# One scan over both row blocks of a pair, and the FFN's units carried on around the out-projection, in a decoder layer on one core

## The chip, the cores and the metric

One core of a Trainium2 chip. The metric is device time in microseconds of one execution of the whole program. TensorE multiplies matrices into PSUM, ScalarE applies functions with a per-partition scale and bias, VectorE and POOL (GpSimd) do elementwise work, and SyncE issues the DMAs. Each engine runs its own instructions in order and waits on semaphores.

## The reference

A decoder layer with three sublayers, each followed by a residual sum and a layer norm, on x of 2 x 2048 tokens x 512:

```python
xz = x @ W_in + b_in;  u, z = silu(first half), silu(second half)      # 1024 channels each
B, C = split(u @ W_xproj + b_xproj);  dt = softplus(u @ W_dt + b_dt)    # 16 states
h = h * exp(dt * A) + (dt * u) * B        # per token, channel and state, in order of time
y = (sum over states of h * C + D * u) * z
x = layernorm(x + y @ W_out + b_out)
x = layernorm(x + cross_attention(x, context of 77 tokens, 16 heads, mask))
hidden = x @ W1 + b1                      # 2048
q = hidden + gain * sin(theta + 0.1 * hidden);  x = layernorm(x + relu(q) @ W2 + b2)
```

## The kernel before

**The scan part** (`selective_scan_phase`). The 4096 tokens are cut into 8 time chunks of `TS` = 512; four chunks make a sequence. In a chunk the 1024 channels x 16 states are 128 row blocks of 128 rows, taken two at a time: 64 pairs a chunk, 512 in all, and every engine's program is one loop over `pair`. The two blocks of a pair lie side by side in PSUM and SBUF, 512 columns each. For one pair:

- TensorE spreads dt over states into `r_ps` (`rep_dt`, L361, four matmuls of 32 rows) and dt*u into `u_ps` (`rep_dtu`, L374). `r_ps` holds two pairs, `u_ps` one.
- ScalarE makes exp(dt*A) in place in `r_ps` (`exps`, L599, one ACTIVATE per block, since the scale differs).
- VectorE multiplies `u_ps` by B into `h` (`dbu`, L743, 1024 columns at once) and runs the recurrence (`scans`, L756, one scan per block, start value from `carry` or zero).
- ScalarE saves the last column of both blocks (`save_carry`, L605), for this pair of the next time chunk; POOL then multiplies `h` by C (`weigh`, L852).
- TensorE sums over states every second pair (`sums`, L390) and, in every fourth of those, adds the D*u row by an identity matmul (L398).

`h` is a ring of three groups of two pairs. The order on the engines is written by hand. TensorE's turn for `pair` is `rep_dtu(pair + 2)`, `produce`, an out-tile's half in the last chunk, `sums`, `rep_dt(pair + 2)`. `produce` holds the projections of the next time chunk, cut by the class `Plan` into 6 or 9 matmuls of 512 columns a pair (L40 to L42 on `pj`, one PSUM bank that ScalarE evacuates). ScalarE's turn is evacuations, `save_carry(pair)`, `exps(pair + 2)`, then Silu with its table loads, softplus and fp16 halves. VectorE's turn is `dbu(pair + 1)`, `scans(pair)`, and a `gate` every eighth pair. In the last chunk pairs 32 to 63 also carry half an out-projection tile each (`out_piece`, 12 matmuls).

**The attention and FFN part** (`attention_ffn_phase`) goes over 16 token chunks of 256. Body c holds the attention of chunk c and the FFN of chunk b = c - 1, and chunks 1 to 6 (`ops`) also the out-projection of two tiles of a later chunk: 48 matmuls of 512 columns into `sps`, the same PSUM that the scores use. The FFN has 8 units: `hidden(b, n)` (24 matmuls of 256 columns), ScalarE's `hid_out`, VectorE's `fraction`, ScalarE's `sine`, VectorE's `mix`, ScalarE's `relu`, VectorE's `act_low`, then `second(b, n)` on TensorE (24 matmuls of 512 columns). ScalarE's `out_evacuated` (L1447) empties the out-projection, VectorE's `masked` (L1710) reads the scores. POOL adds biases (`o_bias`, `x1_bias`, `x1_sum`, `x2_bias`) and makes the low half of y (`y_low`, L1900). Chunk 1 is special (`late` is false): weights are still being split there, and its out-projection's second tile needs `y_low(5)`.

## Time and profile before

| what | value |
|---|---|
| median of 3 runs | 3168.35 us (3167.78 to 3171.23) |
| profiled execution | 3163.83 us |
| its span | 3162.1 us |
| mean granted clock of TensorE | 0.966 |
| scan part: first and last scan start | 59.0 and 1962.9 us |

The span runs from the first to the last instruction of the profiled execution; a clock of 1.0 is 2.4 GHz, 0.5 is 1.2 GHz. Work on an engine that is not waited for costs nothing, so the table says little without the order of waits.

### The profile page before, as it was taken

Reading aid. Unit: us, or ns where it says so; the run is one execution under the profiler, and the core shown is the slowest. Engines: PE = TensorE matmul, PEld = TensorE weight load, DVE = VectorE, ACT = ScalarE, POOL = GpSimd, SP = SyncE. Lnnn points to the kernel's source line nnn. Section 1 sums busy time; section 2 is a strip of 40 time slices with the busy share of each in tenths; the row PEclk is TensorE's granted clock in tenths of the full one; section 3 lists DMA queues with packets and bytes.
Section 4 is the critical chain, followed back from the end, with each engine's and each line's share of the span. In section 5 each row is a group of like instructions: output and inputs, shape, how many; then the busy total and the mean of one; then the engine's idle time right before and its main releaser. Section 6 shows DMA issues by size and latency. Waiting matters only on the chain. (4 is left out here: it accounts for less than half of the span.)

```text
span 3162.1 us, 48953 instructions
## 1 busy us (share of the span) xinstructions
PE 2830.4 (90%) x18968; PEld 1268.4 (40%) x18968; DVE 2692.5 (85%) x3070; ACT 2015.1 (64%) x3616; POOL 1828.9 (58%) x944
## 2 busy tenths in 40 slices
PE   7878878978878888888889889989999999999998
PEld 2222222222222222222222223556666676667765
DVE  5899999999999999999999978766666677777776
ACT  6766776776776776776776745555555556655564
POOL 4788988978978988978988987311111111112100
PEclk9999999999999999999999989999999999999999
DMA  4111112112112111111112143701111000000000
GB/s 159 51 51 41 58 51 66 45 37 71 41 43 65 41 51 57 50 41 57 51 53 65 51 131 125 225 28 42 42 42 42 28 29 22 23 30 29 30 8 14
DMA packets 119976, 172.51 MB, mean 55 GB/s; under 512 B 13250, under 2 KB 48706, under 8 KB 119236
## 3 DMA queue, kind: packets, MB, share of 16 engines
q1 hardware_dynamic: 119748, 169.37, 16.5%
q8 instruction: 155, 2.54, 0.3%
q14 instruction: 73, 0.60, 0.1%
HBM read 100.66 MB, written 66.58 MB: 53 GB/s over the span
## 5 line engine op out<-in xcount | busy, mean ns | idle before, releaser
L852 POOL TENSOR_TENSOR h<-h,c_rep 128x1024 f32<-128x1024 f32 x511 | 1196.7, 2355 | 281.6 <-ACT carry L605 280.1
L756 DVE TENSOR_TENSOR_SCAN h<-r_ps,carry,h 128x512 f32<-128x512 f32 x768 | 938.9, 1262 | 10.6 <-ACT r_ps L599 10.4
L599 ACT ACTIVATE r_ps<-r_ps,decay 128x512 f32<-128x512 f32 x1024 | 631.7, 656 | 390.3 <-PE r_ps L361 389.8
L743 DVE TENSOR_TENSOR h<-u_ps,b_rep 128x1024 f32<-128x1024 f32 x512 | 614.0, 1199 | 48.0 <-PE u_ps L374 47.4
L374 PE MATMUL u_ps<-dtu,spread 32*128 32x512 f16 x2048 | 319.5, 390 | 105.3 <-DVE h L743 105.0
L361 PE MATMUL r_ps<-dt,spread 32*128 32x512 f16 x2048 | 316.9, 387 | 49.7 <-DVE h L756 43.1
L390 PE MATMUL y_ps<-h,gather 128*32 128x512 f32 x2048 | 288.4, 637 | 65.8 <-POOL h L852 64.7
L1882 POOL TENSOR_TENSOR o_in<-o_in,rows 128x1024 f32<-128x1024 f32 x15 | 37.0, 2464 | 508.9 <-DMA o_in<-o_dram 508.9
L756 DVE TENSOR_TENSOR_SCAN h<-r_ps,zero,h 128x512 f32<-128x512 f32 x256 | 313.1, 1263 | 7.1 <-ACT r_ps L599 7.0
L40 PE MATMUL fps<-x,region 128*128 128x256 f16 x1024 | 283.6, 277 | 3.4 <-issue 2.4
L41 PE MATMUL fps<-x,region 128*128 128x256 f16 x1024 | 283.0, 276 | 0.0
L42 PE MATMUL fps<-x,region 128*128 128x256 f16 x1024 | 282.8, 276 | 0.0
L40 PE MATMUL pj<-x_high,region 128*128 128x512 f16 x484 | 194.5, 402 | 39.3 <-ACT u L517 18.6
L361 PEld LDWEIGHTS r_ps<-dt,spread 32*128 32x128 f16 x2048 | 58.2, 93 | 392.5 <-DVE h L756 206.9
L1900 POOL TENSOR_TENSOR y<-y_t,y 128x1024 f16<-128x1024 f32 x13 | 28.3, 2180 | 318.8 <-ACT y L1440 318.8
L40 PE MATMUL pj<-u_high,region 128*128 128x512 f16 x504 | 199.4, 396 | 1.7 <-ACT soft L572 1.4
L40 PE MATMUL nat<-region,act 128*128 128x512 f16 x512 | 194.1, 379 | 7.1 <-DVE act L1695 5.8
L41 PE MATMUL pj<-u_low,region 128*128 128x512 f16 x504 | 197.4, 392 | 0.0
L42 PE MATMUL pj<-u_high,region 128*128 128x512 f16 x504 | 197.1, 391 | 0.0
L42 PE MATMUL nat<-region,act 128*128 128x512 f16 x512 | 194.0, 379 | 0.0
L41 PE MATMUL nat<-region,act 128*128 128x512 f16 x512 | 194.0, 379 | 0.0
L41 PE MATMUL pj<-x_low,region 128*128 128x512 f16 x484 | 192.6, 398 | 0.0
(260 smaller groups left out, 5635.0 us busy)
## 6 DMA issues: line engine op xcount, KB each, us to landing
u_t_dram<-u SPq DMA_DIRECT2D x16, 1024.0 KB, 4.7
uz<-u_t_dram SPq DMA_DIRECT2D x64, 256.0 KB, 4.0
z_t_dram<-zs SPq DMA_DIRECT2D x32, 512.0 KB, 3.0
uz<-z_t_dram SPq DMA_DIRECT2D x64, 256.0 KB, 4.1
y_t_dram<-y SPq DMA_DIRECT2D x64, 256.0 KB, 2.3
region<-y_t_dram SPq DMA_DIRECT2D x32, 256.0 KB, 3.3
result<-x SPq DMA_DIRECT2D x16, 512.0 KB, 2.8
x_t<-dram_x_t SPq DMA_DIRECT2D x15, 512.0 KB, 4.0
```

Of the source, the lines that this page charges most:

```text
L40: nc.tensor.matmul(out, w[0], x[0], start=start, stop=False)
L41: nc.tensor.matmul(out, w[0], x[1], start=False, stop=False)
L42: return nc.tensor.matmul(out, w[1], x[0], start=False, stop=stop)
L361: last = nc.tensor.matmul(r_ps[:, 2 * (pair % 2) + o, :], spread[32 * i:32 * i + 32, p // 2, :], dt16[32 * i:32 * i + 32, s, j, :], start= ...
L374: last = nc.tensor.matmul(u_ps[:, o, :], spread[32 * i:32 * i + 32, p // 2, :], dtu16[32 * i:32 * i + 32, s, j, :], start=(s == 0), stop=( ...
L390: last = nc.tensor.matmul(y_ps[32 * i:32 * i + 32, :], gather[:, q, :], h[:, g % H_GROUPS, i, :], start=(q == 0), stop=(q == 3))
L599: nc.scalar.activation(bank, bank, ACT.Exp, scale=decay[:, col:col + 1]).then_inc(s_da, 1)
L743: nc.vector.tensor_tensor(h[:, g % H_GROUPS, o:o + 2, :], u_ps[:, :, :], b_rep[:, c % 2:c % 2 + 1, :].broadcast_to([P, 2, TS]), ALU.mult). ...
L756: nc.vector.tensor_tensor_scan(row, r_ps[:, 2 * (pair % 2) + o, :], row, start, ALU.mult, ALU.add)\
L852: nc.gpsimd.tensor_tensor(rows, rows, c_rep[:, c % 2:c % 2 + 1, :].broadcast_to([P, 2, TS]), ALU.mult)\
L1882: nc.gpsimd.tensor_tensor(o_in[:, :, :], o_in[:, :, :], row(0), ALU.add).then_inc(s_ob, 1)
L1900: nc.gpsimd.tensor_tensor(y16[:, 1, :, t * P:(t + 1) * P], y_first[i % 2] if i < Y_PAIRED else y_t[:, :, :], y16[:, 0, :, t * P:(t + 1) * ...
```

## The change

In the scan part, a pair's two blocks become one scan of 1024 columns. For that the second block must not take over the first one's state: column 512, the joint column, gets a decay of zero. TensorE writes it, by a matmul of one column of zeros into `r_ps` (`joint_decay_zero`), after the exponentials. In a time chunk that goes on with a sequence, ScalarE has before that added decay x carry to that column of `h` (`joint_column`, right after `exps`). The scan waits for `s_cut` instead of the exponentials. In the second part, chunks with an out-projection run FFN unit 2 right after it, spread the four score groups between later units, and run the sine, relu and VectorE steps of units 0 and 1 during the out-projection's block; in chunk 1 some loads, sums and POOL steps are moved earlier.

```diff
@@ in selective_scan_phase, TensorE
+        no_decay = zero[0:32, :].bitcast(FP16)[:, 0:1]
+        def joints(pair):
+            c = pair // PAIRS
+            return pair - (c // PER_SEQ + 1) * PAIRS
             def rep_dt(pair):
...
-                    pe.wait_ge(s_scan, 2 * pair - 2)
+                    pe.wait_ge(s_scan, pair - 1)
...
+            def joint_decay_zero(pair):
+                c, j, p = place(pair)
+                pe.wait_ge(s_da, 2 * pair + 2)
+                if c % PER_SEQ:
+                    pe.wait_ge(s_joint, joints(pair) + 1)
+                nc.tensor.matmul(r_ps[:, 2 * (pair % 2) + 1, 0:1], spread[0:32, 0, :], no_decay, start=True, stop=True)\
+                    .then_inc(s_cut, 1)
...
                     out_piece((s - OUT_AT) // 2, (s - OUT_AT) % 2)
+                if pair + 1 < TOTAL:
+                    joint_decay_zero(pair + 1)
                 if pair % 2 and pair >= 3:
                     sums((pair - 3) // 2)
@@ ScalarE
+            def joint_column(pair):
+                c, j, p = place(pair)
+                if c % PER_SEQ == 0:
+                    return
+                act.wait_ge(s_da, 2 * pair + 2)
+                act.wait_ge(s_m1, pair + 1)
+                act.wait_ge(s_carry, pair - PAIRS + 1)
+                col = j * NSTATE + 2 * p + 1
+                at = h[:, pair // 2 % H_GROUPS, 2 * (pair % 2) + 1, 0:1]
+                nc.scalar.activation(at, r_ps[:, 2 * (pair % 2) + 1, 0:1], ACT.Identity, bias=at,
+                                     scale=carry[:, col:col + 1]).then_inc(s_joint, 1)
...
                     exps(pair + 2)
+                    joint_column(pair + 2)
@@ VectorE
-                for o in range(2):
-                    col = j * NSTATE + 2 * p + o
-                    dve.wait_ge(s_da, 2 * pair + o + 1)
-                    row = h[:, pair // 2 % H_GROUPS, 2 * (pair % 2) + o, :]
-                    start = carry[:, col:col + 1] if c % PER_SEQ else zero[:, 0:1]
-                    nc.vector.tensor_tensor_scan(row, r_ps[:, 2 * (pair % 2) + o, :], row, start, ALU.mult, ALU.add)\
-                        .then_inc(s_scan, 1)
+                dve.wait_ge(s_cut, pair + 1)
+                o = 2 * (pair % 2)
+                col = j * NSTATE + 2 * p
+                rows = h[:, pair // 2 % H_GROUPS, o:o + 2, :].rearrange("p o t -> p (o t)")
+                start = carry[:, col:col + 1] if c % PER_SEQ else zero[:, 0:1]
+                nc.vector.tensor_tensor_scan(rows, r_ps[:, o:o + 2, :].rearrange("p o t -> p (o t)"), rows, start,
+                                             ALU.mult, ALU.add).then_inc(s_scan, 1)
@@ in attention_ffn_phase, TensorE, a chunk with an out-projection
+                    hidden(b, 2)
                     scores(c, 0, batch, (0, 1), ops)
+                    hidden(b, 3)
+                    scores(c, 0, batch, (2, 3), ops)
+                    second(b, 0)
+                    scores(c, 1, batch, (0, 1), ops)
+                    hidden(b, 4)
+                    scores(c, 1, batch, (2, 3), ops)
+                    second(b, 1)
@@ ScalarE, first body alone
-                    y_high(Y_PAIRED - 1)
                     weights_high(8)
                     weights_high(9)
+                    y_high(Y_PAIRED - 1)
@@ ScalarE, a chunk with an out-projection
+                    if not late:
+                        deviation("x1", 0, c + 2)
+                    sine(b, 0)
                     out_evacuated(m * NT, sps)
+                    sine(b, 1)
+                    relu(b, 0)
+                    relu(b, 1)
                     out_evacuated(m * NT + 1, sps)
+                    hid_out(b, 2)
+                    sine(b, 2)
+                    hid_out(b, 3)
+                    sine(b, 3)
+                    relu(b, 2)
+                    relu(b, 3)
+                    exps(c, 0)
+                    exps(c, 1)
+                    hid_out(b, 4)
@@ VectorE, a chunk with an out-projection
+                    fraction(b, 0)
+                    fraction(b, 1)
+                    if not late:
+                        statistics("x1", 0, c + 1, x1[:, 1 - par, :, :])
+                        normalize("x1", 0, c + 1, x1[:, 1 - par, :, :])
+                    mix(b, 0)
+                    mix(b, 1)
+                    act_low(b, 0)
+                    act_low(b, 1)
                     masked(c, 0, (0, 1))
+                    fraction(b, 2)
...
@@ POOL, before the first body and in it
-                for i in range(1, Y_PAIRED - 1):
+                for i in range(1, Y_PAIRED - 2):
                     y_low(i)
+                o_bias(2)
+                y_low(Y_PAIRED - 2)
...
-                if more:
+                if more and late:
                     pool.wait_ge(s_avl, c * NT)
                     o_bias(c + 1)
...
+                if not late:
+                    for m in ops:
+                        y_low(m * NT + 1)
                 x2_bias(c - 1, 1 - par)
```

SyncE's loads of chunk 2 (`o_in`, `x1`) move with them to before the first body. Line numbers of the kernel after are other ones: L786 is the scan, L389 the one-column matmul, L627 the joint column, L616 the exponentials, L404 and L412 the sums and the D*u row, L367 and L380 the spreads.

TensorE in the scan part, the fourth time chunk, from the projection matmuls of one pair to those of the next, before (`pj` is the projection's bank, `y_ps` the sums over states, `uz` and `ident` the D*u row):

```order
L40 MATMUL pj<-x_high,region 128x512
L41 MATMUL pj<-x_low,region 128x512
L42 MATMUL pj<-x_high,region 128x512
L390 MATMUL y_ps<-h,gather 32x512 x4
L398 MATMUL y_ps<-uz,ident 128x512
L361 MATMUL r_ps<-dt,spread 128x512 x4
L374 MATMUL u_ps<-dtu,spread 128x512 x4
```

and now:

```order
L40 MATMUL pj<-x_high,region 128x512
L41 MATMUL pj<-x_low,region 128x512
L42 MATMUL pj<-x_high,region 128x512
L389 MATMUL r_ps<-zero,spread 128x1
L404 MATMUL y_ps<-h,gather 32x512 x4
L412 MATMUL y_ps<-uz,ident 128x512
L367 MATMUL r_ps<-dt,spread 128x512 x4
L380 MATMUL u_ps<-dtu,spread 128x512 x4
```

The new matmul stands ahead of the sums and of the next spread of dt, and what it waits for holds them up.

ScalarE in the second part, from the evacuation of FFN unit 0 on, in a chunk with an out-projection, before (`units` are the FFN's hidden values, `p_t` the evacuated out-projection, `act` the result of relu, `pr` the scores):

```order
L1470 ACTIVATE units<-fps,turns 128x256 x2
L1474 ACTIVATE units<-fps,b 128x256 x2
L1447 ACTIVATE p_t<-sps 128x512 x2
L1480 ACT_TABLE_LOAD
L1480 ACTIVATE units<-units 128x512
L1470 ACTIVATE units<-fps,turns 128x256 x2
L1474 ACTIVATE units<-fps,b 128x256 x2
L1486 ACTIVATE act<-units 128x512
```

and now, from the same place:

```order
L1512 ACTIVATE units<-fps,turns 128x256 x2
L1516 ACTIVATE units<-fps,b 128x256 x2
L1522 ACT_TABLE_LOAD
L1522 ACTIVATE units<-units 128x512
L1489 ACTIVATE p_t<-sps 128x512
L1522 ACTIVATE units<-units 128x512
L1528 ACTIVATE act<-units 128x512 x2
L1489 ACTIVATE p_t<-sps 128x512
L1512 ACTIVATE units<-fps,turns 128x256 x2
L1516 ACTIVATE units<-fps,b 128x256 x2
```

The table load, both sines and both relus of units 0 and 1 have moved from behind the out-projection's evacuations to between and ahead of them.

## Rows read from the trace of the kernel before

**Rows 1.** Page, part 2: VectorE's busy tenths in 40 equal slices.
```profile
DVE  5899999999999999999999978766666677777776
```

**Rows 2.** Windows: busy us (and instructions) by engine, granted clock, DMA share, GB/s.
```profile
320.00:400.00 80.00, 71.18 (x429) 20.48 (x427) 80.00 (x71) 59.05 (x110) 74.31 (x42) 1.00 0.16 49
1840.00:1920.00 80.00, 77.88 (x465) 26.30 (x468) 68.86 (x62) 40.89 (x76) 65.16 (x39) 0.98 0.43 134
```

**Rows 3.** Lines of the span: busy us, mean ns of one, idle before, releasers.
```profile
L756 DVE TENSOR_TENSOR_SCAN h<-r_ps,carry,h 128x512 f32<-128x512 f32 x768 | 938.9, 1262 | 10.6 <-ACT r_ps L599 10.4
...
L743 DVE TENSOR_TENSOR h<-u_ps,b_rep 128x1024 f32<-128x1024 f32 x512 | 614.0, 1199 | 48.0 <-PE u_ps L374 47.4 <-DVE region L770 0.2
...
L605 ACT ACTIVATE carry<-h 128x2 f32<-128x2 f32 x512 | 102.9, 201 | 55.4 <-DVE h L756 54.7
...
L1690 DVE SCALAR_TENSOR_TENSOR units<-units,gain 128x256 f32<-128x256 f32 x256 | 112.2, 479 | 56.5 <-ACT units L1480 52.7
```

**Rows 4.** Timeline, smooth stretch of the scan part: start, us, engine, line, idle before.
```profile
999.46 1.20 DVE L743 TENSOR_TENSOR h<-u_ps,b_rep 128x1024 f32<-128x1024 f32 x1
...
1000.57 2.44 DVE L756 TENSOR_TENSOR_SCAN h<-r_ps,carry,h 128x512 f32<-128x512 f32 x2
...
1000.71 0.60 PE L374 MATMUL u_ps<-dtu,spread 32*128 32x512 f16 x4 [0.51 <-DVE h L743]
...
1000.97 1.25 ACT L599 ACTIVATE r_ps<-r_ps,decay 128x512 f32<-128x512 f32 x2
...
1002.33 0.38 PE L42 MATMUL pj<-x_high,region 128*128 128x512 f16 x1
...
1004.05 2.44 DVE L756 TENSOR_TENSOR_SCAN h<-r_ps,carry,h 128x512 f32<-128x512 f32 x2
```

**Rows 5.** Timeline around pairs 46 and 47 of the fourth time chunk.
```profile
943.06 1.06 PE L390 MATMUL y_ps<-h,gather 128*32 128x512 f32 x8
...
943.41 1.22 ACT L599 ACTIVATE r_ps<-r_ps,decay 128x512 f32<-128x512 f32 x2
...
945.12 0.39 PE L361 MATMUL r_ps<-dt,spread 32*128 32x512 f16 x2
...
947.01 1.24 ACT L599 ACTIVATE r_ps<-r_ps,decay 128x512 f32<-128x512 f32 x2
...
947.95 2.44 DVE L756 TENSOR_TENSOR_SCAN h<-r_ps,carry,h 128x512 f32<-128x512 f32 x2
```

**Rows 6.** Timeline at pair 1 and pair 55 of the fourth time chunk.
```profile
778.30 1.22 ACT L599 ACTIVATE r_ps<-r_ps,decay 128x512 f32<-128x512 f32 x2
...
779.28 1.27 DVE L756 TENSOR_TENSOR_SCAN h<-r_ps,carry,h 128x512 f32<-128x512 f32 x1
...
977.88 1.24 ACT L599 ACTIVATE r_ps<-r_ps,decay 128x512 f32<-128x512 f32 x2 [5.76 <-PE r_ps L361]
...
979.09 1.27 DVE L756 TENSOR_TENSOR_SCAN h<-r_ps,carry,h 128x512 f32<-128x512 f32 x1
```

**Rows 7.** Windows: a token chunk with an out-projection and one without.
```profile
2162.93:2241.54 78.61, 76.48 (x585) 51.20 (x584) 51.35 (x90) 41.38 (x77) 13.67 (x6) 0.98 0.14 42
2542.81:2608.06 65.25, 64.54 (x536) 45.57 (x536) 49.52 (x90) 38.39 (x73) 9.28 (x4) 1.00 0.08 26
```

**Rows 8.** Timeline of TensorE after an out-projection in token chunk 3.
```profile
2229.13 1.12 PE L1273 MATMUL sps<-k_t,q_t 32*128 32x77 f32 x16 [0.78 <-ACT p_t L1447]
...
2231.26 1.30 PE L1273 MATMUL sps<-k_t,q_t 32*128 32x77 f32 x16 [1.01 <-DVE pr L1710]
...
2232.68 0.42 PE L41 MATMUL fps<-x,region 128*128 128x256 f16 x1
...
2235.57 0.27 PE L40 MATMUL fps<-x,region 128*128 128x256 f16 x1
```

**Rows 9.** Timeline in token chunk 1: POOL's last `y_low`, TensorE's second tile.
```profile
2061.27 2.12 POOL L1900 TENSOR_TENSOR y<-x,y 128x1024 f16<-128x1024 f32 x1
...
2063.44 0.61 PE L40 MATMUL sps<-w_out,y 128*128 128x512 f16 x1 [6.01 <-POOL y L1900]
```

More of the change, by code:

```diff
@@ L1133, in first @@
                 load_piece(7)
+                sp.wait_ge(s_x1, 1)
+                load(o_in[:, :, :], chunk_rows("o", 2), s_oin)
                 store_projection(1, o_out[:, :])
@@ L1807, in body @@
                         weights_low(n)
-                if more:
+                if more and late:
                     statistics("x1", 0, c + 1, x1[:, 1 - par, :, :])
@@ L1915, in body @@
                         y_low(m * NT)
-                if more:
+                if more and late:
                     pool.wait_ge(s_avl, c * NT)
```

122 lines of the change are left out of this document (72 added, 50 removed).

## The prediction

> **What bounds the kernel now.** I read the page first. In its 40 slices of 79 us VectorE shows 9 in slices 3 to 23 and 6 to 8 after, so the kernel has two parts with different limits [rows 1]. The windows say the same: in 320 to 400 us VectorE is busy all 80.00 us and TensorE 71.18, while in the stretch of the out-tiles, 1840 to 1920, TensorE has 77.88 and VectorE 68.86 [rows 2]. Then I read the costliest groups. Per pair of row blocks VectorE does one multiply of 1024 columns (L743) and two scans of 512 (L756), and its idle time before them is small, 48.0 us before the multiplies and 10.6 before the 768 scans with a carry [rows 3]. The timeline gives the beat: multiply at 999.46, scans at 1000.57, the next pair's at 1004.05, so 3.48 us a pair, of which 1.11 is the multiply and 2.37 the two scans [rows 4]. In the first part the end is set by VectorE except where ScalarE or TensorE is late. In the second part TensorE sets it: a token chunk with an out-projection takes 78.61 us with 76.48 busy at a clock of 0.98, one without takes 65.25 with 64.54 at 1.00 [rows 7].
>
> **The merged scan, what it saves.** The trace has no scan of 1024 columns. One scan lasts 1262 ns, two take 2.44, so the second starts 1.18 after the first [rows 3, 4]. If all of that were per column, a scan of 1024 would take 2.36 and save nothing. For the part that is paid per instruction I have the multiply, 1.11 us for 1024 columns, 1.08 ns each [rows 4]. A scan that goes over each column twice would need 1.11 for 512 and leave 0.07. The nearest row with a per-partition operand, as the scan's start value is one, is L1690: 256 of them fill 112.2 us, so two take 0.88, minus 0.48 for the last leaves 0.40 from start to start; 256 columns at 1.08 are 0.28, which leaves 0.12 [rows 3]. I take 0.12, bounds 0 and 0.12: 511 x 0.12 = 61 us, if VectorE stays the bound everywhere. The Trainium skill (VectorE: DVE Perf Modes, The TRN2 errata) puts the measured fixed term at about 150 cycles, paid once by one large tile and per tile by many small ones; at 0.96 GHz that is 0.156 us, an estimate of 80 us by that page. No row here separates the two, and the spacing above speaks for the smaller.
>
> **What the merged scan adds.** The chain ahead of a scan is longer. Before, scan one could start on the first exponential; now the scan waits for `s_cut`, so for both exponentials, in six of eight time chunks for ScalarE's joint column, and for TensorE's one-column matmul. Prices: the second exponential, half of 1.25, so 0.6 after the first [rows 4]; the joint column from the nearest small ACTIVATE, L605, 201 ns plus 0.03 to wait for its own engine, 0.24 [rows 3]; the matmul from L374: it starts 0.05 after the multiply's end and four of 512 columns in two waves 0.22 apart last 0.60, so 0.17 remains as a tail; with a hop on either side 0.25 [rows 4]. Joint and matmul are 0.5 us after the exponentials' end (0.25 in the two chunks that begin a sequence).
>
> In the smooth stretches this is hidden. The exponentials that begin at 1000.97 end at 1002.22 and their scan begins at 1004.05, 1.8 us of cover. The last of six projection matmuls starts at 1002.33, so TensorE is free for the cut at 1002.55, 1.5 us ahead of the scan; with nine matmuls it is 3 x 0.215 less, 0.86, and it needs 0.25 [rows 4]. If that cover is gone, the wait is lost whole, since VectorE has nothing else. I read all pairs for it: where the exponentials end less than 0.5 us before the scan, or TensorE comes to the place of the cut less than 0.25. In the time chunk that begins at 775.8 that is so at nine places, pairs 1, 5 to 7, 25, 29 to 31, 34, 38 to 42, 46 and 47, 50, 54 and 55 (first and last in [rows 6]). Pair 1: exponentials end at 779.52, the cut comes at 780.04, the scan began at 779.28: 0.76 late. Pair 55: they end at 979.12, the cut at 979.64 would be 0.55 late, and it is 0.9 because TensorE's projection matmuls end later still. Of such a pair's lateness VectorE takes off what it idles before a later pair of the same place anyway (2.6 us before pair 55).
>
> The dearest place is pair 46 and 47, and it shows what is queued behind the new wait [rows 5]. The cut of pair 46 stands on TensorE ahead of the sums (L390), the D row (L398) and the spread of pair 47 (L361). Before, the sums ran at 943.06 and the spread at 945.12, 2.06 us later, beside ScalarE's work. Now TensorE waits for the exponentials of 943.41, which end at 944.63, then the joint column, and is free at 945.2; sums and D row take it to 947.2, the spread to 947.9, the exponentials of pair 47 end at 949.2 instead of 948.25, the projection's six matmuls end at 949.6, and the cut comes at 949.85 against a scan that began at 947.95: 1.9 us. Who waits is the scan and all behind it, POOL's `weigh` too. The nine places by the same reading: 0.76, 0.5, 0.3, 0.8, 0.3, 1.25, 1.9, 0.7, 0.95, sum 7.5; each also forgoes the 0.12 that it had gained, 1.1. That is 8.5 us against 64 x 0.12 = 7.7. Per time chunk I put 10 (the first, where start-up work crowds TensorE), 9, 9, 8.5, 6 (no joint column), 9, 7.5 and 10. In the last chunk 32 pairs carry out-tiles, TensorE is the bound there [rows 2], so 32 one-column matmuls are paid in full and nothing is gained. One costs between nothing and the 0.22 of a full one (four last 0.60, one 0.38) [rows 4]; I take 0.1, 3 us. Sum 69 against 61: **+8 us** for the first part. Bounds: if places that follow one another share one delay and the sums' new place costs nothing, about 35, so -26; if every late pair adds its own, as the plain sum of all the lateness in that reading, 100, so +39.
>
> **The FFN chunks.** Chunks 1 to 6 carry an out-projection. In chunks 2 to 6 TensorE stands idle 0.78 us ahead of the scores, for ScalarE's second evacuation (L1447), and 1.01 ahead of the second score group, for VectorE's read (L1710) [rows 8]. Both gaps are where scores follow the out-projection and one another with nothing between. After them matmuls of 256 columns last 0.42 from 2232.68 until at 2235.57 they last 0.27 again: the lower of the two clock levels (1.2 and 2.4 GHz) after an engine that idled and ran small matmuls. 14 matmuls at 0.21 apart instead of 0.108 are 1.5 us more. In the new order hidden unit 2 (24 matmuls at 0.108, 2.6 us) stands between the out-projection and the scores, and hidden 3, second 0 and hidden 4 between the score groups; evacuation and reads, under 1.1 us by the gaps, fit under each. Bound from the rows: 65.25 for a chunk without, plus 48 matmuls at 0.215 = 10.3, is 75.6 against 78.61: 3.0 us a chunk, 15 for five [rows 7]. Next to be late is hidden 6: it needs ScalarE's hid_out 4, now behind both softmax exponentials; counted from the rows' durations it is done within 0.1 us of TensorE's arrival, so I charge nothing. Below: 1.5 a chunk if it is late by that much; above, 3.6.
>
> Chunk 1 has a gap of 6.01 us: the second out-projection tile waits for POOL's `y_low`, at 2061.27 behind bias and sum passes, and TensorE then runs matmuls of 512 columns that last 0.61, not the 0.38 of full clock [rows 4, 9]. With the gap, some 12 matmuls at twice the spacing (2.5) and the same 3.3 as its neighbours that is 11.8. Taking o_bias(2) out of POOL's way and `y_low` ahead of x2_bias brings it some 6 us forward, about when it is wanted. But there ScalarE's evacuations now stand behind deviation, a table load and two sines, all after the last weights: scores wait about 3 us anew, with 1.5 of slow clock. Net 7. **-22 us** for the second part, bounds -10 and -30.
>
> **Sum.** +8 - 22 = -14. The profiled execution took 3163.8 (span 3162.1), so 3149.8 there; the median of the runs shown is 4.5 above it, so **3154 us**.
>
> **Rivals.** (a) The forecast, -14 with -30 to 0 of its own: 0.40. (b) The cover holds: delays overlap with idle time that VectorE has already, 35 instead of 69, or the scan's fixed part is larger; -26 - 22 = -48, 3120. For it speaks that VectorE stalls there anyway; against it the walk through pairs 46 and 47. 0.20. By the 0.156 of the Trainium skill (VectorE: DVE Perf Modes) the forecast would be 3135, which lies in this case. (c) Slower: TensorE's in-order wait for the cut. Sums and spread of every second pair start later by what the exponentials are late, so the next exponentials are late too, and the ring exponentials, joint, cut, sums, spread closes: 1.25 + 0.24 + 0.1 + 1.0 + 0.6 is 3.2 without the D row and 4.3 with it, against 3.36. It decides when the first part's lateness exceeds 61 + 22 = 83 us, 0.16 a pair; at 100 it gives +17, 3185. 0.20. (d) The second part moves its waits instead of losing them (hid_out 4 behind the exponentials, chunk 1): -5, total +3, 3171. 0.15. (e) The scan of 1024 saves nothing: +47, 3215. 0.05.
>
> **Numbers.** Within 0.2% (6 us) is about what a measurement of this kernel cannot tell from no change. Faster by more: 0.33 of (a), all of (b), 0.06 of (d): 0.59. Within: 0.07 of (a), 0.06 of (d), 0.05 of (c): 0.18. Slower: 0.23. The range reaches into (b) and (c): 3122 to 3184.
>
> **What would show it.** L786 with 1024 columns at a start-to-start of 2.24 to 2.25 (right) or 2.36 (e). A beat of 3.36 in smooth stretches. VectorE's idle time before all scans at some 70 to 90 with TensorE's L389 as its releaser; under 50 is (b), over 100 is (c). TensorE idle before L389 for ScalarE, and its sums later. ScalarE's 384 joint columns near 0.2. In chunks 2 to 6 no gap ahead of scores, clock 1.00, 75.6 us from chunk to chunk; a gap before a hidden unit is (d). The last time chunk some 3 us longer. Wrong would also be a first part in which POOL, at 74.31 of 80 busy [rows 2], becomes the bound at the shorter beat.

## The result: slower, 3224.82 us

The changed kernel takes 3224.82 us (median of 4 runs, 3220.13 to 3226.99) against 3168.07 for the kernel before: ratio 1.0177, 95% interval 1.016 to 1.0195. The forecast was 3154, and 3184 was the upper end of its range. The profiled span is 3225.3 us with a clock of 0.959. The last scan ends at 2050.3 us, 86 us later than before; what comes after it takes 1175.0 instead of 1197.9, 23 us less. So the second part did what was forecast (-22), and the whole error is in the scan part (+8 forecast, +86 seen in the profile, +83 in timed runs of that part alone).

The page of the changed kernel, VectorE's busy tenths and the granted clock in 40 slices (here of 81 us), against [rows 1]:

```profile
DVE  6899988988988999988988978776766677777775
...
PEclk9999999989999999989999979999999999999999
```

The row of nines is broken: of slices 3 to 23, all nines in [rows 1], ten are down to 8. The groups say what it waits for. Costliest groups of the changed kernel (busy us, mean ns of one, idle just before them, and what ended it), against [rows 3]:

```profile
L786 DVE TENSOR_TENSOR_SCAN h<-r_ps,carry,h 128x1024 f32<-128x1024 f32 x384 | 899.5, 2342 | 133.1 <-PE r_ps L389 131.1 <-ACT carry L634 1.6 <-DVE h L773 0.3
...
L773 DVE TENSOR_TENSOR h<-u_ps,b_rep 128x1024 f32<-128x1024 f32 x512 | 614.9, 1201 | 37.3 <-PE u_ps L380 36.9 <-DVE region L800 0.2
...
L786 DVE TENSOR_TENSOR_SCAN h<-r_ps,zero,h 128x1024 f32<-128x1024 f32 x128 | 299.7, 2341 | 33.4 <-PE r_ps L389 33.3
L404 PE MATMUL y_ps<-h,gather 128*32 128x512 f32 x2048 | 296.7, 653 | 23.2 <-POOL h L882 22.0 <-DVE h L842 1.1
...
L627 ACT ACTIVATE h<-r_ps,h,carry 128x1 f32<-128x1 f32 x384 | 134.9, 351 | 12.9
...
L389 PE MATMUL r_ps<-zero,spread 32*128 32x1 f16 x512 | 85.0, 166 | 194.9 <-ACT h L627 167.1 <-ACT r_ps L616 24.6
L412 PE MATMUL y_ps<-uz,ident 128*128 128x512 f32 x128 | 83.9, 742 | 0.0
```

VectorE stands idle 166.5 us (133.1 + 33.4) before the merged scans; before the change it was 17.7 for all scans (10.6 of them in [rows 3]). That is +149. Before the multiplies it idles 11 less. The scan itself saves 0.108 us a pair (below), 55 us. 149 - 11 - 55 is 83, close to the loss of 86 (the sum leaves out VectorE's smaller waits). TensorE idles 194.9 us ahead of the new one-column matmul, 167.1 of it for ScalarE's joint column. The sums (L404) and the D row (L412) last 653 and 742 ns; before they lasted 637 and 652.

The timeline of the changed kernel where the exponentials come late (start, duration, idle before):

```profile
1000.47 1.22 ACT L616 ACTIVATE r_ps<-r_ps,decay 128x512 f32<-128x512 f32 x2
...
1001.72 0.35 ACT L627 ACTIVATE h<-r_ps,h,carry 128x1 f32<-128x1 f32 x1
...
1002.22 0.16 PE L389 MATMUL r_ps<-zero,spread 32*128 32x1 f16 x1 [1.59 <-ACT h L627]
...
1002.31 1.06 PE L404 MATMUL y_ps<-h,gather 128*32 128x512 f32 x8
...
1002.51 2.35 DVE L786 TENSOR_TENSOR_SCAN h<-r_ps,carry,h 128x1024 f32<-128x1024 f32 x1 [1.23 <-PE r_ps L389]
```

The exponentials end at 1001.69. Then come 0.03, the joint column 0.35, a hop of 0.15, the matmul 0.16 and a hop of 0.13: 0.82 us to the scan's start, where I had priced 0.5. Counted from the start of the exponentials it is 2.04.

The place that the prediction called the dearest, pairs 46 and 47 of the fourth time chunk, against [rows 5]. The first line is of the kernel before, its D row there; the others are of the changed kernel:

```profile
944.06 1.12 PE L398 MATMUL y_ps<-uz,ident 128*128 128x512 f32 x2
```

```profile
983.10 1.22 ACT L616 ACTIVATE r_ps<-r_ps,decay 128x512 f32<-128x512 f32 x2
...
984.35 0.35 ACT L627 ACTIVATE h<-r_ps,h,carry 128x1 f32<-128x1 f32 x1
...
984.85 0.16 PE L389 MATMUL r_ps<-zero,spread 32*128 32x1 f16 x1 [2.78 <-ACT h L627]
...
984.94 1.06 PE L404 MATMUL y_ps<-h,gather 128*32 128x512 f32 x8
985.14 2.35 DVE L786 TENSOR_TENSOR_SCAN h<-r_ps,carry,h 128x1024 f32<-128x1024 f32 x1 [1.76 <-PE r_ps L389]
...
985.93 2.08 PE L412 MATMUL y_ps<-uz,ident 128*128 128x512 f32 x2
...
987.94 0.60 PE L367 MATMUL r_ps<-dt,spread 32*128 32x512 f16 x2
...
989.02 1.24 ACT L616 ACTIVATE r_ps<-r_ps,decay 128x512 f32<-128x512 f32 x2 [1.85 <-PE r_ps L367]
```

TensorE stands 2.78 us behind the new wait, with the sums, the D row and the next spread queued behind it. The spread starts 3.09 us after the matmul, at 987.94, as soon as the D row is through; the scan that it needs, that of pair 45, had ended at 982.27. The next exponentials can start only after the spread, so the next pair is late as well (0.78 us). The window of the stretch shows the granted clock (PE, PEld, DVE, ACT, POOL busy; clock):

```profile
984.00:990.00 6.00, 5.15 (x23) 1.35 (x24) 3.27 (x2) 4.12 (x7) 4.37 (x3) 0.72 0.43 163
```

Here the wait is paid twice: as idle time, and as the lower clock level (1.2 GHz) for a part of what follows. The D row takes 2.08 us instead of 1.12.

Lengths of the eight time chunks, worked out from the start of each chunk's first scan in the two timelines (the eighth up to the end of its last scan):

| us | 1 | 2 | 3 | 4 | 5 | 6 | 7 | 8 |
|---|---|---|---|---|---|---|---|---|
| before | 249.1 | 233.0 | 234.7 | 235.2 | 232.3 | 235.3 | 232.4 | 253.2 |
| after | 250.6 | 250.9 | 248.9 | 247.3 | 236.4 | 250.0 | 246.9 | 262.5 |

Chunks 1 and 5 begin a sequence and have no joint column: they lose 1.5 and 4.1 us. The other six lose 9 to 18 each.

In the second part, windows of two token chunks with an out-projection in the changed kernel, each with 573 matmuls, 2.1 us short of the whole chunk:

```profile
2195.02:2267.51 72.49, 72.49 (x573) 48.91 (x572) 49.47 (x87) 40.16 (x75) 13.65 (x6) 1.00 0.14 46
2493.60:2566.08 72.48, 72.48 (x573) 48.90 (x572) 49.46 (x87) 40.15 (x74) 13.67 (x6) 1.00 0.11 38
```

The same stretches before, cut the same way:

```profile
2112.69:2189.18 76.49, 74.36 (x573) 49.75 (x572) 49.35 (x87) 39.75 (x74) 13.67 (x6) 0.98 0.14 43
2427.11:2503.60 76.49, 74.36 (x573) 49.96 (x572) 49.36 (x87) 39.75 (x75) 13.67 (x6) 0.98 0.11 37
```

TensorE no longer idles (2.13 us less) and keeps its full clock (busy time for the same 573 matmuls falls by 1.87): 4.0 us a chunk. From one chunk's first softmax exponential to the next chunk's it is 74.6 us instead of 78.6. Chunk 1 gives only 1.6 by the same measure (86.75 instead of 88.36): its 6.01 us gap of [rows 9] is gone, but TensorE waits elsewhere in it.

```profile
2126.73 1.97 PE L1212 MATMUL tr<-ident,x 128*128 128x128 f32 x8 [3.22 <-DVE x L1733]
```

### The profile page after: what moved, and what is told of

Same layout as the page of the kernel before. It is cut to its first block and busy times, and to the rows that moved or that the text cites. A ratio compares the mean times of both kernels' runs of the same rounds, so it can differ in the third digit from the quotient of the medians.

```text
span 3225.3 us, 50616 instructions
## 1 busy us (share of the span) xinstructions
PE 2870.5 (89%) x19480; PEld 1304.8 (40%) x19480; DVE 2652.9 (82%) x2558; ACT 2136.1 (66%) x4000; POOL 1829.2 (57%) x944
## 5 line engine op out<-in xcount | busy, mean ns | idle before, releaser
L786 DVE TENSOR_TENSOR_SCAN h<-r_ps,carry,h 128x1024 f32<-128x1024 f32 x384 | 899.5, 2342 | 133.1 <-PE r_ps L389 131.1
L616 ACT ACTIVATE r_ps<-r_ps,decay 128x512 f32<-128x512 f32 x1024 | 631.7, 656 | 450.3 <-PE r_ps L367 447.9
L380 PE MATMUL u_ps<-dtu,spread 32*128 32x512 f16 x2048 | 328.2, 399 | 69.1 <-DVE h L773 67.1
L367 PE MATMUL r_ps<-dt,spread 32*128 32x512 f16 x2048 | 326.8, 395 | 5.4 <-DVE h L786 2.7
L786 DVE TENSOR_TENSOR_SCAN h<-r_ps,zero,h 128x1024 f32<-128x1024 f32 x128 | 299.7, 2341 | 33.4 <-PE r_ps L389 33.3
L404 PE MATMUL y_ps<-h,gather 128*32 128x512 f32 x2048 | 296.7, 653 | 23.2 <-POOL h L882 22.0
L389 PE MATMUL r_ps<-zero,spread 32*128 32x1 f16 x512 | 85.0, 166 | 194.9 <-ACT h L627 167.1
L389 PEld LDWEIGHTS r_ps<-zero,spread 32*128 32x128 f16 x512 | 46.6, 91 | 436.8 <-ACT r_ps L616 342.3
```

The source lines that it names most:

```text
L367: last = nc.tensor.matmul(r_ps[:, 2 * (pair % 2) + o, :], spread[32 * i:32 * i + 32, p // 2, :], dt16[32 * i:32 * i + 32, s, j, :], start= ...
L380: last = nc.tensor.matmul(u_ps[:, o, :], spread[32 * i:32 * i + 32, p // 2, :], dtu16[32 * i:32 * i + 32, s, j, :], start=(s == 0), stop=( ...
L389: nc.tensor.matmul(r_ps[:, 2 * (pair % 2) + 1, 0:1], spread[0:32, 0, :], no_decay, start=True, stop=True)\
L404: last = nc.tensor.matmul(y_ps[32 * i:32 * i + 32, :], gather[:, q, :], h[:, g % H_GROUPS, i, :], start=(q == 0), stop=(q == 3))
L616: nc.scalar.activation(bank, bank, ACT.Exp, scale=decay[:, col:col + 1]).then_inc(s_da, 1)
L786: nc.vector.tensor_tensor_scan(rows, r_ps[:, o:o + 2, :].rearrange("p o t -> p (o t)"), rows, start, ALU.mult, ALU.add).then_inc(s_scan, 1)
```

## The experiments

Differences in us below are the ratio to the kernel before of the same submission, times 3165. An interval of a ratio is about 0.0017 to either side, 5 us (6 us for the first). Where a kernel is called late at a pair, VectorE idles over 0.3 us before that pair's scan, in the six time chunks that go on with a sequence; chain is the time from the start of a pair's exponentials to its scan there, the median over the late pairs.

### The two parts apart

**e1_ffn_only**: the diff of the second part alone. **e2_scan_only**: the diff of the scan part alone.

> The scan part as before, the attention and FFN part as in the change. Theory: the two parts are independent, and the second alone gives what its trace shows after the last scan, about 22 us: 3146 us. Rival: the second part gains only because the scan part hands over later or in another state; then the gain is off by more than 5 us.

> The scan part as in the change, the second part as before. Theory: all of the loss lies here, 57 + 22 = 79 us: 3247 us. Rival as in the run of the second part alone: under 3240 or over 3255.

Measured: e1 3142.46 (0.9925, 0.9904 to 0.9945), -24. e2 3251.53 (1.0262), +83. The sum, +59, is the whole's +56 within the intervals. The second part is faster than both kernels.

### What in the scan part costs

**e3_no_cut**: merged scan, no joint column, no matmul, so the second block goes on from the first one's state. **e4_cut_no_joint**: with the matmul, no joint column. **e5_two_wait_both**: the kernel before, but the first scan waits for both exponentials. **e6_cut_after_sums**: e2 with the matmul behind the sums.

```diff
 e3 (against e2)
-                    joint_decay_zero(pair + 1)
-                    joint_column(pair + 2)
-                dve.wait_ge(s_cut, pair + 1)
+                dve.wait_ge(s_da, 2 * pair + 2)
 e4 (against e2)
-                if c % PER_SEQ:
-                    pe.wait_ge(s_joint, joints(pair) + 1)
-                    joint_column(pair + 2)
 e5 (against before)
-                    dve.wait_ge(s_da, 2 * pair + o + 1)
+                    dve.wait_ge(s_da, 2 * pair + 2)
 e6 (against e2)
-                if pair + 1 < TOTAL:
-                    joint_decay_zero(pair + 1)
                 if pair % 2 and pair >= 3:
                     sums((pair - 3) // 2)
+                if pair + 1 < TOTAL:
+                    joint_decay_zero(pair + 1)
```

> The scan part of the change without the joint column and without the one-column matmul: one scan of 1024 columns that waits for both exponentials (the second block then starts from the first block's last state, so the recurrence computed is another one). The second part as before. Theory that the chain joint column, matmul, scan is the cost: the scan saves about 0.11 us a pair, less some for the second exponential, so 20 to 50 us under before: 3118 to 3148. Rival, the merged scan itself or its wait for both exponentials is the cost: 3200 or more.

> As the scan part of the change, with the one-column matmul and the wait for it, but without ScalarE's joint column and TensorE's wait for it (the second block then starts from zero in every time chunk). The second part as before. Theory that TensorE's in-order wait for the exponentials is the greater part: 3190 to 3230. Rival, ScalarE's 384 joint columns (0.35 us each) are the greater part: 3140 to 3175.

> The kernel before, with its two scans of 512, but the first scan waits for both exponentials. The run without the cut gained only 5 us, where 511 x 0.11 = 55 were to be had. Theory: the wait for the second exponential gives the other 50 back, so here, without the merged scan's gain, 3205 to 3220 us. Rival: the merged scan's gain is lost to something else, and this wait is nearly free: 3165 to 3180.

> The scan part of the change with the one-column matmul behind the sums and the D row instead of ahead of them; second part as before. Theory: what makes the wait dear is that it stands in TensorE's order ahead of the sums and the D row, which then run late, and at the lower clock level after the idle time: with them ahead 3195 to 3225 us. Rival: the length of the chain exponentials, joint column, matmul, scan alone is the cost, whatever stands behind it: 3240 or more.

| kernel | us | ratio | difference | chain | late scans of 384 |
|---|---|---|---|---|---|
| before | | | 0 | 0.77 | 10 |
| e5_two_wait_both | 3181.73 | 1.006 | +19 | 1.35 | 9 |
| e3_no_cut | 3162.31 | 0.9983 | -5 | 1.35 | 26 |
| e4_cut_no_joint | 3182.17 | 1.005 | +16 | 1.61 | 85 |
| e2_scan_only | 3251.53 | 1.0262 | +83 | 2.06 | 118 |
| e6_cut_after_sums | 3274.84 | 1.0357 | +113 | 4.27 | 137 |

(Chain and late scans are worked out from the start times in each timeline; for the kernels with two scans the first scan of a pair counts.) Of the expectations, e3 (3118 to 3148), e4 (3190 to 3230), e5 (3205 to 3220) and e6 (3195 to 3225) all missed. Groups of the scans in e3, and of the scans and the matmul in e4:

```profile
L782 DVE TENSOR_TENSOR_SCAN h<-r_ps,carry,h 128x1024 f32<-128x1024 f32 x384 | 901.2, 2347 | 32.6 <-ACT r_ps L613 17.2 <-ACT carry L631 12.0
```

```profile
L783 DVE TENSOR_TENSOR_SCAN h<-r_ps,carry,h 128x1024 f32<-128x1024 f32 x384 | 900.9, 2346 | 75.1 <-PE r_ps L387 74.4 <-DVE h L770 0.3 <-ACT carry L632 0.2
...
L387 PE MATMUL r_ps<-zero,spread 32*128 32x1 f16 x512 | 88.3, 172 | 89.4 <-ACT r_ps L614 89.4
```

Two readings. The merged scan gives 24 us (e5 to e3, the same wait for both exponentials), not the 55 that it saves on VectorE: with the shorter beat more scans are late (9 to 26), and VectorE's idle time grows by 16 us before the scans (32.6 to 48.4) and by 16 before the multiplies (41.5 to 57.5). And the price is small for the matmul (+21) and large for the joint column (+67).

e6 fell the other way than I had expected. My reading was that TensorE's wait ahead of the sums costs, so I had expected 3195 to 3225 from moving it behind them. It was slower. Behind the sums, the matmul comes when TensorE is through with them, and the scan waits for the matmul: half of the late scans are 4.27 us or more behind their exponentials' start. TensorE stands still for POOL ahead of the sums only 11 us of the whole; mostly it is its own queue that holds the matmul up. This run puts a new delay in the place of the old one, so it does not decide the question.

### What the joint column's price consists of

**e7_joint_unwaited**: e4 with two small ACTIVATEs on SBUF under the joint column's waits, which nobody waits for. **e8_zero_by_scalar**: ScalarE writes the zero itself, behind the joint column, and TensorE has no matmul. **e9_one_unwaited**: as e7 with one ACTIVATE. **e10_before_one_small**: the same ACTIVATE in the kernel before. **e11_waits_only**: only its waits.

```diff
 e9 (against e4; e7 has two of them, e11 the waits alone, e10 is the same in the kernel before)
+                act.wait_ge(s_da, 2 * pair + 2)
+                act.wait_ge(s_m1, pair + 1)
+                act.wait_ge(s_carry, pair - PAIRS + 1)
+                nc.scalar.activation(spare[:, n:n + 1], d_skip[:, 0:1], ACT.Identity,
+                                     bias=d_skip[:, 1:2], scale=d_skip[:, 2:3])
 e8 (against e2)
-                    joint_decay_zero(pair + 1)
+                nc.scalar.activation(at, at, ACT.Copy, scale=0.0).then_inc(s_cut, 1)
```

> As the run with the matmul and without the joint column, but in its place ScalarE runs two small ACTIVATEs on constants, with the joint column's waits, for which nobody waits (the second block starts from zero). Two of them take ScalarE about 0.22 us, the joint column 0.25 from start to start. Rival, ScalarE's occupancy makes up the 69 us of the joint column: 3225 or more. Theory, that it is the wait of TensorE for it, in the ring of exponentials, joint column, matmul, sums and spread: 3180 to 3200.

> The scan part of the change, but ScalarE itself writes the zero into the joint column of the decays, by a small ACTIVATE with scale 0 behind the joint column, and the scan waits for that; TensorE has no one-column matmul and no wait. Second part as before. Theory that TensorE's in-order wait is the cost: 3185 to 3215 us, in spite of 512 more small ACTIVATEs. Rival, the chain and ScalarE's time are the cost: 3240 or more.

> The scan part alone, with TensorE's one-column matmul, which waits for the exponentials only; in the joint column's place ScalarE does one small ACTIVATE of the same form under the same three waits, on SBUF operands and into a spare column that nobody reads. So the first state of each second row starts from zero in place of the saved carry. No engine waits for the small ACTIVATE. Known: 3182 without it, 3252 with the real joint column, 3227 with two such ACTIVATEs, which took 0.57 us of ScalarE a pair. Theory A (latency: the 0.82 us from the exponentials' end to the scan is what costs, and of it the joint column's 0.35): near 3182, at most 3195. Rival B (occupancy: ScalarE is full in the long stretches, and 0.25 to 0.30 us more for each of 320 pairs costs, whoever waits): half of the 45 of the two, so near 3205, and up to 3252 if it is the whole of the joint column's price.

> The kernel before, two scans of 512 columns a pair and the second part as before, with one small ACTIVATE a pair on ScalarE behind the second exponential, under the waits that the joint column has, into a spare column that nobody reads. The output is computed as before. It prices ScalarE's occupancy alone, without any longer chain to the scan. Theory A: the exponentials come up to 0.3 us later only where ScalarE works without a pause; 3175 to 3190. Rival B: 320 pairs by 0.28 us are 90 us of ScalarE, which sets the pace in most of a time chunk; 3210 to 3250. No cost at all (3167) would say that ScalarE has the room everywhere, and that the joint column costs by its latency alone.

> The scan part alone with TensorE's one-column matmul, and on ScalarE only the joint column's three waits (both exponentials ended, the product ready, the carry saved) with no ACTIVATE behind them. The first state of each second row starts from zero in place of the saved carry. It prices what ScalarE loses by waiting until its own exponential has drained, in order, ahead of its next instruction. Theory A and rival B both: within 8 us of the 3182 without the waits, since each wait is shorter than 0.1 us. Rival C (the product comes late, so that ScalarE stands still behind this wait and the next exponentials start late): 3195 to 3230.

Measured: e7 3227.32 (1.0203), +64. e8 3241.12 (1.0243), +77. e9 3202.22 (1.0121), +38. e10 3188.62 (1.0073), +23. e11 3191.72 (1.0079), +25. The small ACTIVATEs in e9:

```profile
L626 ACT ACTIVATE spare<-d_skip 128x1 f32<-128x1 f32 x384 | 148.6, 387 | 12.9
```

e7's two took 0.57 us of ScalarE a pair, more than twice the joint column's, so by itself it overstated occupancy; its expectation had put 0.22. Both e7 and e8 fell where the rival had them, that ScalarE's time and the chain are the cost, and not where the wait of TensorE alone would have put them (3180 to 3200 and 3185 to 3215). With one small ACTIVATE the steps are: waits +9 (e4 to e11, where at most 8 had been expected), the ACTIVATE's time +13 (e11 to e9), and +45 more when engines wait for it (e9 to e2). In the kernel before, the same ACTIVATE costs 23 with its waits, where e9's costs 22. e8 has no matmul and no wait on TensorE, and is yet only 6 us better than e2: its second small ACTIVATE starts 0.44 us after the joint column and lasts 0.16, so ScalarE has e7's load. But e7, which has the matmul and in which nobody waits for the two, costs 64. In e8 110 scans are late at a chain of 2.00 us, and VectorE idles 117.8 us before the scans with a carry, though TensorE waits neither for the joint column nor for the zero:

```profile
L793 DVE TENSOR_TENSOR_SCAN h<-r_ps,carry,h 128x1024 f32<-128x1024 f32 x384 | 900.0, 2344 | 117.8 <-ACT r_ps L632 71.0 <-ACT carry L638 45.9 <-DVE h L780 0.3
```

Of the 82 us from e3 to e8 the small ACTIVATEs and their waits account for 48 when nobody waits for them (e4 to e7); some 34 are left for the scan's wait at the end of the longer chain. So the longer chain is dear even where TensorE does not wait for it.

### Who waits for the joint column

**e12_joint_between**: the decay of the joint column is made ahead by a one-column Exp into SBUF, and the joint column stands between the two exponentials; the matmul waits for the exponentials alone, and VectorE for the joint column. **e13_joint_beside**: the joint column reads a constant column, TensorE doesn't wait for it, VectorE does.

```diff
 e12 (against e2)
 # the waits of TensorE and VectorE changed as in e13
+                    nc.scalar.activation(early[:, pair % 2:pair % 2 + 1], r_ps[:, 2 * (pair % 2) + 1, 0:1], ACT.Exp,
+                                         scale=decay[:, col:col + 1]).then_inc(s_early, 1)
                 for o in range(2):
+                    if o and c % PER_SEQ:
+                        joint_column(pair)
 e13 (against e2)
 # TensorE, ahead of the one-column matmul
-                if c % PER_SEQ:
-                    pe.wait_ge(s_joint, joints(pair) + 1)
 # ScalarE
-                nc.scalar.activation(at, r_ps[:, 2 * (pair % 2) + 1, 0:1], ACT.Identity, bias=at,
+                nc.scalar.activation(at, d_skip[:, 0:1], ACT.Identity, bias=at,
 # VectorE, ahead of the scan
+                    dve.wait_ge(s_joint, joints(pair) + 1)
```

> The scan part alone, nothing left out of the computation, with the joint column taken off the chain: ScalarE first makes the decay of that one column by a small ACTIVATE with Exp into SBUF, then the first exponential, then the joint column from the small one's result, then the second exponential. TensorE's one-column matmul waits for the exponentials only. ScalarE's work grows by two small ACTIVATEs for each of 384 pairs in place of one; the chain from the exponentials' end to the scan goes back from 0.82 to near 0.45 us. Known: 3252 with the joint column on the chain, 3182 with none, 3202 with none but its waits and occupancy. Theory A (being waited for costs 49 us, occupancy 10 for each small ACTIVATE, the waits 10): 3182 plus two occupancies plus part of the waits, 3200 to 3222. Rival B (what costs is what ScalarE does for the joint column, so two such ACTIVATEs are worse than one): 3252 or more.

> The scan part alone, with the joint column placed as in the change, behind the second exponential, but it reads a constant column of SBUF in place of the new decay, so that it can run beside TensorE's one-column matmul instead of ahead of it; the scan waits for both. So the decay of the joint column is wrong in value and everything else is computed. ScalarE does the same work. Before a late scan the chain, counted from the start of the exponentials, falls from 2.04 to 2.06 us (joint column, hop, matmul, hop in a row) to 1.24 + 0.03 + 0.38 + 0.13 = 1.78. Amended theory (each us of chain, counted from the exponentials' start, costs some 95 to 100 us when ScalarE's work is the same; taken from 3202 at 1.59 and 3252 at 2.05): 3220, between 3212 and 3230. Rival B (what costs is the joint column's work and its being waited for by anyone, wherever it stands, as the run with the joint column between the exponentials might be read too): 3245 to 3255. Rival C (only TensorE's wait for ScalarE costs, VectorE's does not): 3200 to 3208.

Measured: e12 3251.16 (1.0282), +89, a miss of my theory. e13 3205.61 (1.0131, 1.0114 to 1.0148), +41, some 42 below e2. The timeline of e12 shows the miss:

```profile
1003.92 0.26 ACT L617 ACTIVATE early<-r_ps,decay 128x1 f32<-128x1 f32 x1 [1.68 <-PE r_ps L369]
...
1004.08 0.65 ACT L624 ACTIVATE r_ps<-r_ps,decay 128x512 f32<-128x512 f32 x1
...
1004.65 0.38 ACT L635 ACTIVATE h<-early,h,carry 128x1 f32<-128x1 f32 x1
...
1004.93 0.66 ACT L624 ACTIVATE r_ps<-r_ps,decay 128x512 f32<-128x512 f32 x1
...
1005.64 0.17 PE L389 MATMUL r_ps<-zero,spread 32*128 32x1 f16 x1 [0.35 <-ACT r_ps L624]
```

The chain behind the exponentials was shorter, but the work had only moved in front of the second one: from the spread's release at 1003.92 to the matmul are 1.72 us, against 1.76 in e2. A chain has to be counted from the event that releases it. I then formed the theory that this length, exponentials' start to scan, is the price, and e13 was to confirm it at 3212 to 3230. Its chain was 1.79 as expected, but it cost 3 us more than e9, not 18; the rival that only TensorE's wait counts had said 3200 to 3208, and hit. Neither account fits all the runs: that rival does not fit e8. Scans and matmul in e13:

```profile
L786 DVE TENSOR_TENSOR_SCAN h<-r_ps,carry,h 128x1024 f32<-128x1024 f32 x384 | 900.0, 2344 | 102.5 <-PE r_ps L387 50.6 <-ACT h L625 28.5 <-ACT carry L632 22.6
...
L387 PE MATMUL r_ps<-zero,spread 32*128 32x1 f16 x512 | 88.4, 173 | 106.2 <-ACT r_ps L614 105.9
```

### The order on TensorE

**e14_spread_cut_sums**: e2 with the spread of pair + 2 first, then the matmul of pair + 1, then the sums. **e15_before_spread_first**: the kernel before with the spread ahead of the sums. **e16_ffn_spread_first**: e1 with that order.

```diff
 e14 (against e2)
+                if pair + 2 < TOTAL:
+                    rep_dt(pair + 2)
                 if pair + 1 < TOTAL:
                     joint_decay_zero(pair + 1)
                 if pair % 2 and pair >= 3:
                     sums((pair - 3) // 2)
-                if pair + 2 < TOTAL:
-                    rep_dt(pair + 2)
```

> The scan part alone, whole computation, with another order on TensorE: the spread of pair + 2 first (it waits for the scan of this pair), then the one-column matmul of pair + 1, then the sums. The joint column stays ahead of that matmul. Known: 3252 with matmul, sums, spread in that order; 3206 when TensorE does not wait for the joint column. Theory D (TensorE's in-order wait for the joint column ahead of sums and spread is what costs): the spread no longer stands behind that wait, and the 1.1 us multiply between two scans covers the matmul; 3205 to 3230, or better if the sums' new place costs nothing. Rival (what counts is the chain from exponentials to scan, unchanged here at 2.05 us): 3245 or more, and worse yet if the sums, now later, hold up the ring of h.

> The kernel before with one thing changed: TensorE's spread of pair + 2 ahead of the sums instead of behind them. The control for the run with spread, matmul, sums. Either way of counting expects little, 3155 to 3190: in the smooth stretches the spread then waits for the scan (sums 1.1 us later), in the stalls it no longer waits for POOL's multiplies that the sums wait for.

> The second part of the change, the scan part of before with two scans a pair, and TensorE's spread ahead of the sums. The two measured alone gave -24 and -6 us; they lie in different parts of the program, so they should add: 3136 to 3141. If the spread's -6 was only the spread of its runs (3155 to 3176), 3142 to 3146.

Measured: e14 3225.09 (1.0179), +57, 26 below e2. e15 3158.59 (0.9982, 0.9968 to 0.9996), -6 (between -1 and -10). e16 3136.67 (0.9913, 0.9899 to 0.9927), -28, the fastest of all. Scans and matmul in e14:

```profile
L786 DVE TENSOR_TENSOR_SCAN h<-r_ps,carry,h 128x1024 f32<-128x1024 f32 x384 | 900.4, 2345 | 123.2 <-PE r_ps L389 119.4 <-ACT carry L634 1.0 <-DVE h L773 0.4
...
L389 PE MATMUL r_ps<-zero,spread 32*128 32x1 f16 x512 | 83.6, 163 | 24.5 <-ACT h L627 23.1 <-ACT r_ps L616 1.3
```

TensorE's idle time ahead of the matmul falls from 194.5 to 24.5 us, and its mean clock rises to 0.972, but VectorE's before the scans with a carry only from 136.1 to 123.2. So with the spread out from behind the wait some 20 us come back beyond the order's own 6. The rest is not the old wait left over: e14's chain is no longer 2.06 but 4.43 us (median), and at 74 of its 110 late scans it is over 3. There the exponentials are done long before, and the matmul is held up by TensorE's own queue, the projection matmuls and now the spread as well, not by a wait (24.5 us in all). e14 too puts a new delay in the place of the old one.

## Why the prediction was wrong

**The step that failed** is "What the merged scan adds": 69 us of lateness against 61 gained. What the runs put in its place, as steps from before to the change of the scan part, each with some 7 us of uncertainty:

| step | runs | us |
|---|---|---|
| first scan waits for the second exponential too | before to e5 | +19 |
| one scan for two | e5 to e3 | -24 |
| one-column matmul | e3 to e4 | +21 |
| waits for exponentials, product and carry on ScalarE | e4 to e11 | +9 |
| ScalarE's time for one small ACTIVATE | e11 to e9 | +13 |
| VectorE waits for it, beside the matmul (chain 1.79) | e9 to e13 | +3 |
| TensorE's matmul waits for it, ahead of sums and spread (chain 2.06) | e13 to e2 | +42 |
| sum | | +83 |

The steps of 3 and 9 are no larger than their uncertainty or hardly so. In the prediction's own terms the step failed in the size of the chain (0.5 priced, 0.82 measured), in ScalarE's time, which had no term, and in how much lateness follows from both. How the last 42 us divide between TensorE's wait, the longer chain and the clock stays open.

Point by point:

- **Saved per scan: right.** I took 0.12 us; the beat of the smooth stretches is 3.373 us against 3.48 in [rows 4], so 0.108. The Trainium skill's measured term of 150 cycles (VectorE: DVE Perf Modes, The TRN2 errata), 0.156 us as I had worked it out, is not what this scan shows. But "if VectorE stays the bound everywhere" was not so: of 55 us 24 arrived.
- **The chain's size: too small.** 0.5 priced, 0.82 measured. I took the joint column's 0.24 from a copy of two columns with no operand per partition [rows 3]; with a scale and a bias per partition it lasts 351 ns. The matmul with a hop on either side took 0.44 (0.15 + 0.16 + 0.13), where I had put 0.25. The Trainium skill has the price (ScalarE: Activation LUTs, What ACT_TABLE_LOAD costs): 186 ns fixed and about 93 ns more for each such operand, which makes an estimate of 373 for a scale and a bias; the runs show 351 with its source in PSUM and 385 to 387 in SBUF, so it agrees within 6%.
- **How much the size explains: about half.** It can be counted in the trace of before. For each of the 384 pairs with a carry, take the time from the start of its exponentials to the moment at which VectorE is free for its scan; where a chain is longer, the scan would be late by the difference. For the priced chain (1.75 with both exponentials) that gives 68 us, for the measured one of 2.06 it gives 103, with 110 scans over 0.3 us late; the changed kernel has 133 us and 118. My reading of nine places a time chunk had put 53 for these six chunks (3 of it for the out-tiles' matmuls). For the experiments the count gives 31 at a chain of 1.35 (e3 measured 33), 54 at 1.61 (e4 75), 73 at 1.79 (e13 103) and 103 at 2.06 (e2 136). So the count fits without a matmul on TensorE and falls short by 21 to 33 us with one, and of the 34 us between e13 and e2 it gives 31. It is a count and no experiment.
- **ScalarE's own time: left out.** I charged the joint column as a wait only. Its waits and its time cost 22 us though no engine waits for it (e4 to e9), and 23 in the kernel before (e10).
- **Who waits: counted once, where a part comes back.** I took each place's lateness from the timeline of before and let it end there. The wait for ScalarE stands on TensorE ahead of the spread that the next exponentials need, so at some places a late pair makes the next one late. Pairs 46 and 47 show it. Up to the end of TensorE's wait my walk was right (free 1.8 us after the exponentials' start, measured 1.84). Sums and D row then took 3.0 us where I had 2.0, since the D row ran at the lower clock level, and the exponentials of pair 47 started 5.92 us after those of pair 46, where I had 4.6. From the scan of pair 45 to that of pair 48 it is 14.53 us instead of 10.44, so 4.1 more; I had forecast 1.9. But most of the loss is not such a repetition: of e2's 118 late scans 36 come right behind another late one, and the count above finds nearly as many late scans with no repetition at all. In sum the lateness was 138 us (83 + 55), not 69. The ring is the mechanism of rival (c), which I gave 0.20 and priced at +17. The runs bear it out only in part: e14, which takes the spread out from behind the wait, gives 20 us back, and puts another delay in.
- **The 42 us from e13 to e2: not divided.** Between them TensorE begins to wait for the joint column, the chain to the scan grows from 1.79 to 2.06, and the mean clock falls from 0.966 to 0.954. That TensorE's wait is the cause would fit e13, which came out 6 us under the range of the account by the chain alone; that it is not needed is what e8 shows, +77 without it, at a chain of 2.00 and a clock of 0.947. No run changes one of the three and leaves the other two.
- **The out-tiles: +3 forecast, not seen apart.** The eighth time chunk as a whole went from 253.2 to 262.5 us, 9 more, which is no more than the others lost.
- **The FFN chunks: right in sum, off in parts.** Forecast 3.0 for each of five and 7 for chunk 1; measured 4.0 and 1.6, -24 in e1. The gaps are gone, the clock is 1.00 and hidden 6 doesn't wait. The slow matmuls had cost 1.9 us a chunk rather than 1.5. In chunk 1 a new wait of 3.22 us stands ahead of the transposes; the one that I had forecast ahead of the scores, 3 us, is 2.59.

## What to carry to other kernels

Merging two instructions on the busiest engine pays only what is not waited for again; before pricing the saving, list each new wait on another engine and what is queued behind it there. Then price the longer chain against the cover of every pair, not of a few places: here 0.3 us more of chain was 35 us more of counted lateness. A wait on the engine that also feeds the next round can close a ring, and then that price is a lower bound. Of work that is slipped into a full engine count its time as well as its latency; and measure a chain from its release, not from the last link.

## What the runs showed of the hardware

- A one-column ACTIVATE is not cheap: 351 ns (PSUM source, scale and bias per partition), 385 to 387 (SBUF source, the same), 258 (Exp with a scale per partition).
- The merged scan of 1024 columns lasts 2341 to 2347 ns, the scan of 512 lasts 1262: 1.08 us for 512 columns more, 2.1 ns each.
- A matmul of one column and 32 rows lasts 163 to 173 ns in the profile. From the joint column's end to the matmul's start are 0.15 us, from the matmul's end to the scan's start 0.13.
- After 2.78 us in which TensorE stood still, the D row's two matmuls took 2.08 us, against 1.12 before. In the scan part alone (e2) a pause of 2.71 us ahead of the one-column matmul of pair 38 was followed by this window, with the clock at 0.57, so near the lower level:

```profile
948.00:952.00 4.00, 3.81 (x15) 0.83 (x19) 2.35 (x1) 2.52 (x4) 2.37 (x2) 0.57 0.30 117
```
